# A state-space mixer on one Trainium2 core: silus and taps moved between slots, rounded output weights moved to GpSimd

## The chip, the cores and the metric

The kernel runs on one core of a Trainium2 chip. The metric is the device time of one launch in microseconds. The time before is 2786.01 us, the median of three runs (2781.27 to 2787.26).

## The reference

Four layers run one after the other on 1024 tokens (4 sequences of 256) of width 512: a selective scan, a mixture of experts, a mixer of the Mamba-2 kind and a feed-forward layer with block quantisation. Each is between layer norms and is added to the residual. The change touches the mixer only, which is cut here to what matters:

```python
proj = h @ in_proj_w.T                      # gate 8192, hidden 8192, B 1024, C 1024, dt 128
hBC = silu(causal_conv(hBC, conv_w, conv_b))  # 4 taps along time
hid, B, C = ...                             # 128 heads of 64; 8 groups of B and C, 128 wide
M = einsum('bcihn,bcjhn->bcijh', Ch, Bh) * L  # L = exp of differences of cumulated decays
Y = M @ (hid * dt) + D * hid                # (also across chunks)
yg = Y * silu(gate)
yg = yg * rsqrt(mean(yg * yg over a group) + EPS) * gnorm_w
out = residual + yg @ out_proj_w.T
```

The heads share B and C within a group: group g has 16 heads, which are 8 pairs of 2 heads, 128 channels a pair.

## The kernel before

The mixer (`mixer_groups`) goes over 72 steps: in each of 8 groups, first a step for B and C, then 8 steps, each for one pair (its hidden channels and its gate). The engines work through slots; in slot s the projections of step s are made, while the pair of step s - 1 is turned into y. With r = s % 9, slot r = 0 projects B and C of a new group and finishes the last pair of the old one, slot r = 1 projects the first pair and has no pair to finish, and slots r = 2 to 8 have both. In slots r = 1 to 4 of groups 1 to 7, TensorE also makes two tiles of 128 tokens of the group before's output (`out_tiles`), and in slots r = 5 to 8 two blocks of output weights are prepared for this group (`new_out_weights`): `wogh`, the weight times `gnorm_w`, rounded to the fp32r type, by ScalarE at L1674 (`high_weight`), and `wogl`, the rest, by VectorE at L1532 (`low_weight`). Every product in fp32r is three matmuls (L78, L79, L80) of rounded and remaining parts.

Each engine has a fixed order, written out in its loop over slots; semaphores tie them together.

TensorE in a slot with a pair: transposes of the pair's hidden channels (L1337, `turn`) for the first half of the tokens, projection 0 (12 matmuls of 512 columns), transposes for the second half, projection 1, the y matmuls of sequence 0 (L1354 and L1358), an out tile if there is one, projection 2, y of sequence 1, projection 3, the second out tile, then y of sequences 2 and 3. The four projections of a step go through three PSUM banks (`mg_pb`) in turn, so projection n waits until the bank's content of three projections ago was read: by the last tap for hidden, B and C, by the silu for the gate. One PSUM bank (`mg_tb`) serves both the transposes and the out tiles; each waits until the one before was emptied (`s_hc`, `s_acc`).

In slot r = 1 TensorE makes projections 0 and 1, the square sums of the finished group (L1380), the shared kernels (B times C of the group, L1372 and L1373, four sequences, in banks of `mg_gb` and `mg_py`), out tile, projection 2, half of projection 3, out tile, and the other half.

ScalarE makes the first tap of the convolution (L1608), the silus (L1618, L1625), the clamps of the decay differences for some sequences (L1639, L1640), the exponentials (L1652, L1658), the rounded halves `yh` (L1667) and `wogh`. The first tap of the second half waits until the product of the pair two steps back was read from the same buffer, by `gated(last, 1)` on GpSimd (L1268).

VectorE makes the other three taps (L1453, `taps`), the product with dt out of the transposes' bank (L1471, `times_step`), the kernels of the eight units of a pair (L1480, `kernel_of`: exponential times shared kernel), the remaining clamps (L1494, L1496), `skip` (L1503, y plus D times hidden), `low` (L1519), `low_weight`, and the sum of out tiles (L1527, `add`). The last y matmuls of a slot need kernels 6 and 7, which are behind `skip(p, 0)` and, in slot r = 0, behind the taps of C's first half.

GpSimd splits the projection weights of the next step (`split`: `wh` at L1256, `wl` at L1258), multiplies y with the silu of the gate (L1268, `gated`) and gathers squares (L1279, L1283, L1285). Its order in a slot is: `split(s + 1)`, second half of the pair before (`gated(last, 1)`, `squares(last, 1)`), first half of this slot's pair. In slot r = 1 the second half comes ahead of the split.

SyncE issues all loads: `mg_ws` (projection weights, one buffer), `mg_abc` (rows of decays), `mg_wos` (output weights, two buffers, L1248).

## Time and profile before

| what | value |
| --- | --- |
| median of 3 runs | 2786.01 us (2781.27 to 2787.26) |
| the profiled execution, its own time | 2787.32 us |
| its span on the core | 2785.5 us |
| granted TensorE clock, mean | 0.936 of full |
| the mixer's groups | about 915 to 2440 us |

The profile shows one execution. Its span runs from the first to the last instruction; the time has 1.8 us around it. Busy times are of instructions alone; waiting isn't busy. In a timeline an instruction's idle time before it, with the instruction that released it, stands in brackets. DVE is VectorE, ACT ScalarE, POOL GpSimd, PE TensorE.

### The profile page before, as it was taken

Reading aid. Unit: us, or ns where it says so; the run is one execution under the profiler, and the core shown is the slowest. Engines: PE = TensorE matmul, PEld = TensorE weight load, DVE = VectorE, ACT = ScalarE, POOL = GpSimd, SP = SyncE. Lnnn points to the kernel's source line nnn. Section 1 sums busy time; section 2 is a strip of 40 time slices with the busy share of each in tenths; the row PEclk is TensorE's granted clock in tenths of the full one; section 3 lists DMA queues with packets and bytes.
Section 4 is the critical chain, followed back from the end, with each engine's and each line's share of the span. In section 5 each row is a group of like instructions: output and inputs, shape, how many; then the busy total and the mean of one; then the engine's idle time right before and its main releaser. Section 6 shows DMA issues by size and latency. Waiting matters only on the chain. (4 is left out here: it accounts for less than half of the span.)

```text
span 2785.5 us, 35722 instructions
## 1 busy us (share of the span) xinstructions
PE 2347.3 (84%) x11172; PEld 1667.8 (60%) x11172; DVE 1986.3 (71%) x3392; ACT 1475.5 (53%) x3113; POOL 1240.7 (45%) x932
## 2 busy tenths in 40 slices
PE   5966667777342899999999999999999999888997
PEld 4531111225332667777767767767777777568996
DVE  4559999994426587686686685776765866778777
ACT  2344444443102596685695685765856956842221
POOL 1129989993000364353363462543543633641122
PEclk9989999998575899999999999999999999889999
DMA  2030030000131331231231221322322312220110
GB/s 78 24 122 0 0 121 0 0 0 31 57 121 64 94 124 60 72 114 54 74 117 48 87 92 53 105 73 65 108 64 68 112 53 75 82 77 24 46 46 31
DMA packets 117376, 183.57 MB, mean 66 GB/s; under 512 B 9760, under 2 KB 77728, under 8 KB 116192
## 3 DMA queue, kind: packets, MB, share of 16 engines
q1 hardware_dynamic: 117216, 181.55, 20.3%
q8 instruction: 86, 1.41, 0.2%
q14 instruction: 74, 0.61, 0.1%
HBM read 170.90 MB, written 10.62 MB: 65 GB/s over the span
## 5 line engine op out<-in xcount | busy, mean ns | idle before, releaser
L78 PE MATMUL mg_pb<-xT2h,mg_wh 128*128 128x512 f32 x1152 | 483.0, 419 | 18.2 <-POOL mg_wl L1258 18.2
L79 PE MATMUL mg_pb<-xT2l,mg_wh 128*128 128x512 f32 x1152 | 458.4, 398 | 0.0
L1268 POOL TENSOR_TENSOR mg_y<-mg_hT,mg_sg 128x512 f32<-128x512 f32 x128 | 175.5, 1371 | 634.5 <-DVE mg_hT L1503 634.5
L80 PE MATMUL mg_pb<-xT2h,mg_wl 128*128 128x512 f32 x1152 | 456.5, 396 | 0.0
L778 PE MATMUL ss_y<-ss_pr,cst 128*128 128x512 f32 x512 | 294.8, 664 | 125.4 <-POOL ss_pr L763 116.5
L763 POOL TENSOR_TENSOR ss_pr<-ss_h,ss_bc 128x512 f32<-128x512 f32 x256 | 328.4, 1287 | 38.6 <-DVE ss_h L731 29.3
L1453 DVE SCALAR_TENSOR_TENSOR mg_hT<-mg_pb,mg_cw,mg_hT 128x510 f32<-128x510 f32 (+2 forms) x432 | 314.2, 740 | 32.3 <-ACT mg_hT L1608 26.5
L1480 DVE TENSOR_TENSOR mg_m<-mg_gb,mg_cb 128x384 f32<-128x384 f32 x512 | 265.2, 549 | 74.7 <-ACT mg_gb L1658 72.1
L662 ACT ACTIVATE ss_da<-dt,ss_na 128x510 f32 (+1 forms) x256 | 175.9, 689 | 210.3 <-DVE ss_h L731 210.2
L778 PEld LDWEIGHTS ss_y<-ss_pr,cst 128*128 128x128 f32 x512 | 80.7, 194 | 338.0 <-POOL ss_pr L763 330.5
L78 PEld LDWEIGHTS mg_pb<-xT2h,mg_wh 128*128 128x128 f32 x1152 | 220.4, 191 | 80.2 <-issue 18.8
L80 PEld LDWEIGHTS mg_pb<-xT2h,mg_wl 128*128 128x128 f32 x1152 | 219.9, 191 | 52.2
L79 PEld LDWEIGHTS mg_pb<-xT2l,mg_wh 128*128 128x128 f32 x1152 | 220.6, 191 | 40.2
L1658 ACT ACTIVATE mg_gb<-mg_nd 128x256 f32<-128x256 f32 x512 | 190.0, 371 | 71.5 <-DVE mg_nd L1496 70.5
L731 DVE TENSOR_TENSOR_SCAN ss_h<-ss_da,ss_dbx 128x512 f32<-128x512 f32 x192 | 226.4, 1207 | 0.0
L1354 PE MATMUL mg_py<-mg_m,mg_hc 128*64 128x256 f32 x1024 | 170.2, 411 | 54.5 <-DVE mg_m L1480 54.4
L1527 DVE SCALAR_TENSOR_TENSOR acc<-mg_tb,mg_rs,acc 128x512 f32<-128x512 f32 x56 | 41.9, 748 | 211.7 <-PE mg_tb L80 211.7
L1652 ACT ACTIVATE mg_gb<-mg_abc,mg_tabs 128x128 f32<-128x128 f32 x512 | 182.7, 357 | 3.8 <-DVE mg_m L1480 2.1
L78 PE MATMUL mg_tb<-mg_wogh,mg_yh 128*128 128x512 f32 x448 | 180.0, 402 | 0.0
L1258 POOL TENSOR_TENSOR mg_wl<-mg_ws,mg_wh 128x1024 fp32r<-128x1024 f32 x72 | 176.0, 2445 | 6.0
L80 PE MATMUL mg_tb<-mg_wogh,mg_yl 128*128 128x512 f32 x448 | 177.0, 395 | 0.0
L1608 ACT ACTIVATE mg_hT<-mg_pb,mg_cbias,mg_cw 128x512 f32<-128x512 f32 x144 | 110.8, 770 | 124.7 <-PE mg_pb L80 113.7
(291 smaller groups left out, 5323.3 us busy)
## 6 DMA issues: line engine op xcount, KB each, us to landing
mg_abc<-acs_rows SPq DMA_DIRECT2D x256, 256.0 KB, 3.3
mg_ws<-in_w_in SPq DMA_DIRECT2D x72, 512.0 KB, 3.6
ss_bc<-bc_rows SPq DMA_DIRECT2D x16, 1024.0 KB, 8.5
mg_wos<-in_w_out SPq DMA_DIRECT2D x64, 256.0 KB, 4.0
ff_ws<-in_w SPq DMA_DIRECT2D x7, 1024.0 KB, 4.8
x<-in_x SPq DMA_DIRECT2D x16, 256.0 KB, 4.3
ip_ws<-in_w_in SPq DMA_DIRECT2D x8, 512.0 KB, 3.6
x_kept<-x SPq DMA_DIRECT2D x2, 2048.0 KB, 7.2
```

The lines of the kernel that those rows point to most:

```text
L78: pe.matmul(out, lhs[0], rhs[0], start=start, stop=False)
L79: pe.matmul(out, lhs[0], rhs[1], start=False, stop=False)
L80: return pe.matmul(out, lhs[1], rhs[0], start=False, stop=stop)
L662: act.activation(da[n % RA][:].rearrange("p (b t) -> p b t", t=SEQ)[:, :, 1:], src[:, :, 1:], ACT.Exp, scale=na[:, bass.ds(k, 1), n:n + 1] ...
L731: dve.tensor_tensor_scan(hh[n % RA][:], da[n % RA][:], src[:], 0.0, ALU.mult, ALU.add).then_inc(s_h, 1)
L763: pool.tensor_tensor(pr[n % 2][:], hh[n % RA][:], bcb[:, NST + n, :], ALU.mult).then_inc(s_pr, 1)
L778: pe.matmul(yb[:], ident, pr[n % 2][:], start=False, stop=n == NST - 1).then_inc(s_y, 1)
L1258: pool.tensor_tensor(wl[s % 2][:], ws[:], wh[s % 2][:].bitcast(F32), ALU.subtract).then_inc(s_lo, 1)
L1453: i = dve.scalar_tensor_tensor(out=d3, in0=s3, scalar=w[:, TAPS - 1 - k:TAPS - k], in1=d3, op0=ALU.mult, op1=ALU.add)
L1480: dve.tensor_tensor(mm[u % 4][:], gb[u % 2][:, 0:BLK], cbt[:, u // 2, :], ALU.mult).then_inc(s_m, 1)
L1652: act.activation(gb[u % 2][:, 2 * P:BLK], abc[(BATCH * p + b) % 3][:, hh, P:SEQ], ACT.Exp, bias=tabs[g % 2][:, 2, 2 * b, 2 * q + hh:2 * q ...
L1658: act.activation(gb[u % 2][:, 0:2 * P], nd[u % 4][:], ACT.Exp, scale=1.0 if by_dve(p, b) else -1.0).then_inc(s_e, 1)
```

## The change

Two things change in the mixer.

First, the work on B and C. In slot r = 0, VectorE makes only the taps of B (the two halves 0 and 1); the taps of C (2 and 3) are made at the start of slot r = 1, around `low` of the first out tile. ScalarE makes all first taps in slot r = 0, those of C behind the exponentials 6 and 7, and all four silus of B and C in slot r = 1. TensorE makes the shared kernels in slot r = 1 behind projection 2 instead of behind projection 1, and projection 3 in one piece ahead of the second out tile; VectorE takes them (`shared_out`) behind `low` of the second out tile.

Second, `wogh` is made by GpSimd, by a multiplication with the column of `gnorm_w` and an addition of 0. Its first weight of a slot stands ahead of `split(s + 1)`, the second between `split(s + 1)` and `gated(last, 1)`.

```diff
--- before.py
+++ after.py
@@ -1284,14 +1284,26 @@
                     pool.wait_ge(s_sqt, n + 1)
                     pool.tensor_tensor(ssq[:, t], ssq[:, t], sq[:], ALU.add).then_inc(s_sq, 1)
 
+                def high_weight(w):
+                    pool.wait_ge(s_wo[w % 2], 16 * (w // 2) + 16)
+                    if w >= PAIRS:
+                        pool.wait_ge(s_out, w // PAIRS * MT)
+                    pool.tensor_scalar(wogh[:, w % PAIRS, :], wos[w % 2][:], gn[:, w:w + 1], 0.0, ALU.mult, ALU.add
+                                       ).then_inc(s_wog, 1)
+
+                pool.wait_ge(s_tab, 64)
                 split(0)
                 for s in range(NSTEP + 2):
-                    last = turned_pair(s - 1) if s else None
+                    last, ow = turned_pair(s - 1) if s else None, new_out_weights(s)
+                    if ow:
+                        high_weight(ow[0])
                     if last is not None and (s % PS == 1 or s > NSTEP):
                         gated(last, 1)
                         squares(last, 1)
                     if s + 1 < NSTEP:
                         split(s + 1)
+                    if ow:
+                        high_weight(ow[1])
                     if last is not None and not (s % PS == 1 or s > NSTEP):
                         gated(last, 1)
                         squares(last, 1)
@@ -1423,16 +1435,15 @@
                     proj(s, 1, 1)
                     if outs:
                         square_sums(s // PS - 1)
-                    if not is_bc(s):
-                        shared_kernels(s // PS)
-                    if outs:
                         out_tile(*outs[0])
                     proj(s, 2, 0)
                     proj(s, 2, 1)
+                    if not is_bc(s):
+                        shared_kernels(s // PS)
                     proj(s, 3, 0)
+                    proj(s, 3, 1)
                     if outs:
                         out_tile(*outs[1])
-                    proj(s, 3, 1)
                 square_sums(NG - 1)
 
             @block.vector
@@ -1567,30 +1578,29 @@
                             add(*outs[0])
                             low(*outs[1])
                         skip(p, 0)
-                        if bc:
-                            taps(s, 2)
                         kernel_of(p, 6)
                         kernel_of(p, 7)
                         if outs:
                             add(*outs[1])
                         skip(p, 1)
-                        if bc:
-                            taps(s, 3)
                         continue
                     if bc:
-                        for j in range(4):
-                            taps(s, j)
+                        taps(s, 0)
+                        taps(s, 1)
                         continue
+                    taps(s - 1, 2)
                     if outs:
                         low(*outs[0])
+                    taps(s - 1, 3)
                     taps(s, 0)
                     if outs:
                         scales(outs[0][0])
                     taps(s, 1)
-                    shared_out(s // PS)
                     if outs:
                         add(*outs[0])
                         low(*outs[1])
+                    shared_out(s // PS)
+                    if outs:
                         add(*outs[1])
                 scales(NG - 1)
                 dve.wait_ge(s_rs, NG)
@@ -1667,45 +1677,32 @@
                         ins = act.activation(yh[:, q0:q1, :], yb[:, r0:r0 + q1 - q0, m * P:(m + 1) * P], ACT.Copy)
                     ins.then_inc(s_yh, 1)
 
-                def high_weight(w):
-                    act.wait_ge(s_wo[w % 2], 16 * (w // 2) + 16)
-                    if w >= PAIRS:
-                        act.wait_ge(s_out, w // PAIRS * MT)
-                    act.activation(wogh[:, w % PAIRS, :], wos[w % 2][:], ACT.Copy, scale=gn[:, w:w + 1]).then_inc(s_wog, 1)
-
                 def root(g):
                     act.wait_ge(s_ss, g + 1)
                     act.activation(sd[:], gb[1][:, BLK:BLK + MT], ACT.Sqrt, bias=eps[:, 2:3], scale=1.0 / GRP
                                    ).then_inc(s_sd, 1)
 
                 for s in range(NSTEP + 1):
-                    p, outs, ow = turned_pair(s), out_tiles(s), new_out_weights(s)
+                    p, outs = turned_pair(s), out_tiles(s)
                     bc = is_bc(s)
                     if p is not None:
                         decay(p, 0)
                         decay(p, 1)
                         if outs:
                             high(*outs[0])
-                        if ow:
-                            high_weight(ow[0])
                         first_tap(s, 0)
                         decay(p, 2)
                         decay(p, 3)
                         first_tap(s, 1)
                         decay(p, 4)
                         decay(p, 5)
-                        if ow:
-                            high_weight(ow[1])
-                        if bc:
-                            first_tap(s, 2)
                         if outs:
                             high(*outs[1])
                         decay(p, 6)
                         decay(p, 7)
-                        if bc and s < NSTEP:
+                        if bc:
+                            first_tap(s, 2)
                             first_tap(s, 3)
-                            for j in range(4):
-                                silu(s, j)
                             continue
                         silu(s, 0)
                         silu(s, 1)
@@ -1715,16 +1712,17 @@
                     if bc:
                         for j in range(4):
                             first_tap(s, j)
-                        for j in range(4):
-                            silu(s, j)
                         continue
                     if outs:
                         high(*outs[0])
+                    silu(s - 1, 0)
+                    silu(s - 1, 1)
+                    silu(s - 1, 2)
                     first_tap(s, 0)
+                    silu(s - 1, 3)
+                    first_tap(s, 1)
                     if outs:
                         root(outs[0][0])
-                    first_tap(s, 1)
-                    if outs:
                         high(*outs[1])
                     silu(s, 0)
                     silu(s, 1)
```

## Rows read from the trace of the kernel before

**Rows 1.** The page: busy time of each engine, and TensorE's clock in 40 slices.

```profile
PE 2347.3 (84%) x11172; PEld 1667.8 (60%) x11172; DVE 1986.3 (71%) x3392; ACT 1475.5 (53%) x3113; POOL 1240.7 (45%) x932
...
PEclk9989999998575899999999999999999999889999
```

**Rows 2.** Busy time of each engine, 1200 to 1300 us; then granted clock, DMA share, GB/s.

```profile
1200.00:1300.00 100.00, 93.70 (x496) 70.48 (x495) 77.12 (x129) 72.44 (x164) 54.49 (x40) 0.97 0.27 86
```

**Rows 3.** Who waited for whom, 1000 to 2450 us: total us, times, longest.

```profile
PE mg_py L1354 <- DVE mg_m L1480: 52.5, 35, 3.8
...
ACT mg_hT L1608 <- POOL mg_y L1268: 10.1, 23, 0.5
```

**Rows 4.** TensorE's timeline: start us, us, instruction, [idle before it <-releaser].

```profile
1251.20 0.65 PE L1354 MATMUL mg_py<-mg_m,mg_hc 128*64 128x256 f32 x4 [0.85 <-DVE mg_m L1480]
...
1270.75 1.12 PE L1354 MATMUL mg_py<-mg_m,mg_hc 128*64 128x256 f32 x4 [3.78 <-DVE mg_m L1480]
...
1272.23 0.80 PE L78 MATMUL mg_pb<-xT2h,mg_wh 128*128 128x512 f32 x1
...
1276.21 0.40 PE L78 MATMUL mg_pb<-xT2h,mg_wh 128*128 128x512 f32 x1
...
1279.65 1.84 PE L1380 MATMUL mg_gb<-cst,mg_ssq 128*128 128x1 f32 x16
...
1299.13 0.40 PE L80 MATMUL mg_tb<-mg_wogh,mg_yl 128*128 128x512 f32 x1
...
1300.76 0.60 PE L1337 MATMUL mg_tb<-cst,mg_hT 128*128 128x128 f32 x4
...
2417.72 0.65 PE L1354 MATMUL mg_py<-mg_m,mg_hc 128*64 128x256 f32 x4
```

**Rows 5.** VectorE's timeline, slots r = 0 and r = 1.

```profile
1252.15 0.75 DVE L1503 SCALAR_TENSOR_TENSOR mg_hT<-mg_hT,mg_dp,mg_py 128x512 f32<-128x512 f32 x1 [1.00 <-PE mg_py L1358]
...
1266.81 0.74 DVE L1503 SCALAR_TENSOR_TENSOR mg_hT<-mg_hT,mg_dp,mg_py 128x512 f32<-128x512 f32 x1
1267.46 2.30 DVE L1453 SCALAR_TENSOR_TENSOR mg_sg<-mg_pb,mg_cw,mg_sg 128x510 f32<-128x510 f32 x3
1269.68 1.01 DVE L1480 TENSOR_TENSOR mg_m<-mg_gb,mg_cb 128x384 f32<-128x384 f32 x2
...
1277.08 4.24 DVE L1519 TENSOR_TENSOR mg_yl<-mg_y,mg_yh 128x256 fp32r<-128x256 f32 x2 [1.74 <-ACT mg_yh L1667]
...
1299.57 0.75 DVE L1527 SCALAR_TENSOR_TENSOR acc<-mg_tb,mg_rs,acc 128x512 f32<-128x512 f32 x1 [7.18 <-PE mg_tb L80]
```

**Rows 6.** Timelines of GpSimd, VectorE and ScalarE in a weight slot, r = 8.

```profile
1237.38 1.06 POOL L1256 TENSOR_SCALAR mg_wh<-mg_ws 128x1024 fp32r<-128x1024 f32 x1
1238.52 2.40 POOL L1258 TENSOR_TENSOR mg_wl<-mg_ws,mg_wh 128x1024 fp32r<-128x1024 f32 x1
1240.87 1.75 POOL L1268 TENSOR_TENSOR mg_y<-mg_hT,mg_sg 128x512 f32<-128x512 f32 x1
...
1239.31 2.16 DVE L1532 SCALAR_TENSOR_TENSOR mg_wogl<-mg_wos,mg_gn,mg_wogh 128x512 fp32r<-128x512 f32 x1
...
1245.67 1.01 DVE L1480 TENSOR_TENSOR mg_m<-mg_gb,mg_cb 128x384 f32<-128x384 f32 x2
...
1242.72 0.78 ACT L1608 ACTIVATE mg_hT<-mg_pb,mg_cbias,mg_cw 128x512 f32<-128x512 f32 x1 [0.44 <-POOL mg_y L1268]
...
1245.46 0.37 ACT L1658 ACTIVATE mg_gb<-mg_nd 128x256 f32<-128x256 f32 x1
```

**Rows 7.** GpSimd's timeline at the end of slot r = 0.

```profile
1267.62 1.26 POOL L1268 TENSOR_TENSOR mg_y<-mg_hT,mg_sg 128x512 f32<-128x512 f32 x1 [6.26 <-DVE mg_hT L1503]
...
1270.08 1.27 POOL L1285 TENSOR_TENSOR mg_ssq<-mg_ssq,mg_sq 128x512 f32<-128x512 f32 x1
```

**Rows 8.** GpSimd's instruction groups, whole span: xcount, busy us, mean ns, idle before.

```profile
L1256 POOL TENSOR_SCALAR mg_wh<-mg_ws 128x1024 fp32r<-128x1024 f32 x72 | 75.7, 1052 | 199.6 <-PE mg_pb L80 158.1 <-DMA mg_ws<-in_w_in 41.6
...
L1035 POOL MEMSET st_go<- 128x4 f32 x1 | 0.1, 104 | 0.1
```

## The prediction, made blind

> **What bounds the kernel now.** I read the page first. TensorE is busy 84% of the span, the other engines 45 to 71%, and its clock is at full level over most of the second half [rows 1]. The mixer's groups fill about 915 to 2440 us of the span. In a stretch of 100 us there, TensorE is busy 93.7 us and no other engine 80 [rows 2]. So TensorE sets the time, and only its gaps, and any microsecond at the lower of its two levels (1.2 GHz instead of 2.4), can be won. The table of waits names one large reason for the gaps: the last y matmul of a slot (L1354) waits for the kernels that VectorE makes at L1480, 52.5 us in 35 waits [rows 3]. The timeline divides them. Seven waits of about 3.76 us (26 us) end the slots with r = 0; 24 waits of about 0.84 us (20 us) end the slots with r = 5 to 8, in which output weights are made (four in group 0; r = 6, 7, 8 in groups 1 to 6; r = 6 and 7 in group 7). One row of each kind stands in [rows 4]. After a long wait TensorE is at the lower level: its nine projection matmuls from 1272.23 to 1276.21 us come every 0.44 us, the next 15, to 1279.65, every 0.23 [rows 4].
>
> **Part 1: C's taps leave slot r = 0.** VectorE ends skip(p, 0) at 1267.46, then makes the three taps of C's first half (2.2 us), and only then kernels 6 and 7, from 1269.68 to 1270.69; TensorE starts 0.06 later [rows 4, 5]. Without the taps the kernels start at 1267.46 and the last y matmuls at 1268.53. The gap shrinks by 2.2 us to 1.56. A gap of 0.85 leaves the clock up and one of 3.78 doesn't [rows 4]. I take 1.56 as harmless, by the nearer one; the rivals have the other end.
>
> I now follow slot r = 1 from there, at full clock. The y matmuls take 0.80 (1251.20 to the transposes at 1252.00), 24 projection matmuls 24 x 0.233 = 5.6, and everything from the square sums on, out tiles and shared kernels included, 1300.76 - 1279.65 = 21.1 [rows 4]. Their sum doesn't change with their order. What changes are the waits:
> - Projection 1 of the slot needs the bank whose taps are now late. skip(p, 1) starts 0.95 after the last y matmuls, as at 1252.15 after 1251.20 [rows 4, 5], so at 1269.48; the moved taps run from 1270.14 to 1272.36. TensorE is there at 1269.33 + 2.8 = 1272.1. Cost 0.3.
> - Square sums need GpSimd's three instructions on the second half of the last pair. GpSimd is busy with the first half until 1270.08 + 1.27 = 1271.35; its three take 3.73 (1267.62 to 1271.35) [rows 7], so alone 1275.1. But low of the first out tile now asks at 1272.4, between them. That is a subtraction of two SBUF tiles; at 1277.08 two such took 4.24 us beside GpSimd's work [rows 5], so the two engines shut each other out. With its 1.2 us slipped in, GpSimd ends at 1276.3; TensorE is there at 1275.2. Cost 1.0, between 0 (no collision) and 1.2.
> - The second out tile now ends the slot. Before, six projection matmuls (1299.37 to 1300.76) covered the add that empties its bank: add starts at 1299.57 and takes 0.75 [rows 4, 5]. After, the transposes of the next slot wait for it: 1300.4 instead of 1299.37. Cost 1.0.
> - The silus of B and C and the four first taps stay ahead of the shared kernels by several us, since these now follow the first out tile and projection 2 (8.4 us); VectorE's waits for them fall into time in which it idles now (7.18 us before the row at 1299.57 [rows 5]). Cost 0. The cover is the first out tile: without it the shared kernels would wait for silu(s - 1, 3).
>
> So slot r = 2 starts at 1268.53 + 0.80 + 5.6 + 21.1 + 0.3 + 1.0 + 1.0 = 1298.3 instead of 1300.76: 2.4 us won per group, 3.4 without the collision. It happens seven times: 17 us, up to 24. Group 0 has no out tile and wins nothing; at its start B and C come in the same order on VectorE.
>
> **Part 2: rounded output weights by GpSimd.** ScalarE loses 64 x 0.71 us, which is worth little: behind its first weight it waits for GpSimd (0.44 us, [rows 6]), behind the second for VectorE's clamps. GpSimd gains two instructions in each of 32 slots. The trace has none of their size. The same operation on 1024 columns takes 1.05 us, an instruction on 4 columns 0.10 [rows 8]; so 512 columns take 0.53 (half) to 0.58 (fixed part kept). I take d = 0.575. The far bound is 1.05, an instruction no shorter for half the columns. The Trainium skill (GPSIMD Engine Reference, 3.1) gives GpSimd two software dispatch steps and puts VectorE's dispatch alone at 156 ns; an estimate with 0.16 as the fixed part would be 0.60, and the sum 1 us worse.
>
> Now a weight slot [rows 6]. GpSimd has wh at 1237.38, wl at 1238.52, and then gated(last, 1) at 1240.87, which takes 1.75 instead of 1.26 because VectorE's low_weight holds it off. gated ends at 1242.62, and ScalarE's first tap of the second half, which overwrites what gated reads, starts 0.10 later. Then come clamps and exponentials; the last one ends at 1245.83, and VectorE's kernel 5 (the second of the pair at 1245.67) starts at 1246.13. The slack between the two is 0.30, or 0.24 with the usual 0.06 of handover. After the change both weights stand ahead of gated(last, 1): it ends 2d = 1.15 later, and kernel 5 is 1.15 - 0.24 = 0.91 later. The other path is shorter: low_weight waits for wl to end (2.16 us instead of its own 0.74), and wl moves by d = 0.575 only. Behind kernel 5 VectorE has clamps, taps, the second low_weight, skip and kernels 6 and 7 without a gap up to TensorE's wait. So each of the 24 stalls grows by 0.91, to 1.75: 21.8 us.
>
> The other eight weight slots keep their time: r = 5 of groups 1 to 7, where the first weight must now wait for the last out tile but ScalarE waits for projection 1 anyway, and the last slot, which has no split and shows no stall today (2417.72, [rows 4]). The DMAs are the same; a weight is asked for 1 to 2 us earlier than by ScalarE, inside the time it has now. The next load of projection weights starts 0.6 us later, up to 4.6 in r = 5; it has most of a slot to spare. GpSimd's added wait for the tables at its start covers what split(0) waits for anyway. Cost 0.
>
> **Sum.** 21.8 - 17.0 = +4.8 us. The profiled execution took 2787.3 (span 2785.5); the median of the runs shown is 1.3 lower, so 2786.0 + 4.8 = 2790.8, rounded to 2791. With d of 0.53 to 0.65 the loss is 0.82 to 1.06 per slot (20 to 25 us) and the gain 12 (further small waits at the first out tile) to 24: 2782 to 2799.
>
> **Rival A, the port goes to VectorE first.** VectorE asks for the port at 1239.31, 0.8 after wl starts. If d is over 0.79, wl hasn't begun by then; low_weight goes first, wl waits about 0.5, and gated ends 1.6 (d = 0.8) to 2.1 (d = 1.05) later: 1.35 to 1.83 per slot, 32 to 44 us, so 2801 to 2813, about 2806. For it: the scalar is read from a column of a tile here, not given as a constant as at L1256. Against: a time proportional to columns puts d well below. The Trainium skill (SBUF — State Buffer, two separate sides) has the first to start keep the shared pair for its whole instruction, which would turn the order at this same point; that the wl row and low_weight end together agrees.
>
> **Rival B, faster: GpSimd's delay is absorbed.** The place is the handover from gated(last, 1) to the first tap. If ScalarE, relieved of 0.6 us ahead of it, or VectorE's order hides the delay, the growth per slot is 0 to 0.5 and the gain of part 1 stays: 2769 to 2781, about 2775. It decides at a growth of 17 / 24 = 0.71 us per slot. Against: ScalarE already waits for gated in 23 places, 10.1 us [rows 3], so relief ahead of it only lengthens that wait.
>
> **Rival C, the clock falls anyway.** Gaps of 1.6, 0.3 and 1.0 now lie within 8 us. The fall costs 8.90 - 6.4 = 2.5 us a time (1270.75 to 1279.65 against 0.80 + 5.6, [rows 4]); seven times is 17 us and brings the time to about 2808. Against: the gaps of 0.85, one a slot, don't do it, and matmuls fill the time between.
>
> **How the numbers follow.** The forecast has 0.47, rival A 0.18, rival B 0.27, rival C 0.08. Both signs hold weight, so the likeliest case's own range is 2782 to 2799. The range to hold 8 in 10 reaches over B and most of A: 2770 to 2809. A measurement of this kernel tells 0.2% (5.6 us) from nothing. Faster by more: B, 0.26. Within it: a good half of the forecast, 0.32. Slower: the rest of the forecast, A and C, 0.42.
>
> **What would show it.** Right: TensorE's wait ahead of the last y matmuls about 1.5 us at r = 0 with the clock up, and about 1.75 in 24 weight slots; ScalarE's wait for gated (L1268) up from 0.4 to over 2 us; a new gap of 1 us ahead of L1337 in slot r = 2, and one ahead of L1380; GpSimd's new group at 0.55 to 0.6 us. Wrong: stalls of 0.8 unchanged in the weight slots, a new group over 0.8 us, or long rows of 0.63 at r = 0.

## The result and the profile after

| | before | after |
|---|---|---|
| median of 5 runs | 2786.01 us (2781.27 to 2787.26) | 2800.01 us (2797.43 to 2803.30) |
| ratio, 95% interval | | 1.0054 (1.0040 to 1.0069) |
| the profiled execution | 2787.32, span 2785.5 | 2800.01, span 2798.2 |

The change makes the kernel 0.5% slower. The forecast was 2791.0 within 2770 to 2809: the sign and the range hold, and the size is three times too small.

The page of the kernel after, to be set beside [rows 1]:

```profile
PE 2351.4 (84%) x11172; PEld 1667.0 (60%) x11172; DVE 1952.2 (70%) x3392; ACT 1440.2 (51%) x3049; POOL 1289.4 (46%) x996
...
PEclk9989999998575999999999999999999999989999
```

TensorE's busy time is what it was (2351 against 2347 us). ScalarE lost its 64 instructions, GpSimd has 64 more and 49 us more work, and the span grew by 12.7 us. So the time is again in TensorE's gaps, and in what its clock does around them. The table of waits, 1000 to 2450 us (who waited for whom: total us, times, longest):

```profile
PE mg_py L1366 <- DVE mg_m L1491: 51.1, 31, 2.7
ACT mg_hT L1618 <- POOL mg_y L1268: 43.2, 23, 2.3
...
PE mg_tb L1349 <- DVE acc L1538: 6.5, 7, 0.9
...
PE mg_gb L1392 <- POOL mg_ssq L1285: 2.8, 7, 0.5
PE mg_pb L78 <- DVE mg_sg L1464: 0.6, 4, 0.2
```

TensorE's wait for kernels has the same sum as in [rows 3] (51.1 against 52.5 us), but made up differently: nothing reaches 3.8 us any more, and the many small ones have grown. ScalarE's wait for gated went from 10.1 to 43.2 us, over 23 places in both. The last three rows are the bill for part 1: the kernel before has no such waits in slots r = 0 and 1 (its one wait for square sums, 5.0 us, stands behind the last group).

To see where each microsecond lies I measured slots. A slot runs from the first transposes (L1337 before, L1349 after) behind one pair's last y matmuls to those behind the next pair's. The table is worked out from their starts in TensorE's timeline, in us:

| stretch | before | after | difference |
|---|---|---|---|
| up to the first projection | 915.3 | 912.3 | -3.0 |
| from there to slot r = 2 of group 0 | 27.3 | 26.5 | -0.8 |
| the 24 weight slots that stall | 399.4 (16.64 each) | 428.2 (17.84) | +28.8 |
| slots r = 0 and 1 together, 7 times | 340.5 (48.65) | 329.7 (47.09) | -10.9 |
| all other slots, the last one too | 736.0 | 736.0 | 0.0 |
| behind them | 367.0 | 365.6 | -1.4 |
| sum | 2785.5 | 2798.2 | +12.7 |

Part 2 costs 28.8 us, and part 1 wins 10.9 in slots r = 0 and 1. The 0.8 us at the start of group 0 isn't shown to be the change's: that stretch took 25.9 to 27.4 us over the kernels of this study, and e4 and e9, which have part 1, took 27.3 and 27.4. The first stretch holds nothing of the change, and over the thirteen kernels of this study it came out anywhere from 909 to 916 us; it is scatter of single executions. The last stretch was 365.4 to 365.7 in all but two kernels (before and e8_low_late, 367.0 and 366.7), which I can't explain. Single spans carry up to 7 us of this, so the mechanisms below are read from slots, and the medians only check them. The slots too are those of one profiled execution of each kernel.

### The profile page after: what moved, and what is told of

Read it like the earlier page. It is cut to its first block and busy times, and to the rows that moved or that the text cites. A ratio compares the mean times of both kernels' runs of the same rounds, so it can differ in the third digit from the quotient of the medians.

```text
span 2798.2 us, 35723 instructions
## 1 busy us (share of the span) xinstructions
PE 2351.4 (84%) x11172; PEld 1667.0 (60%) x11172; DVE 1952.2 (70%) x3392; ACT 1440.2 (51%) x3049; POOL 1289.4 (46%) x996
## 5 line engine op out<-in xcount | busy, mean ns | idle before, releaser
L78 PE MATMUL mg_pb<-xT2h,mg_wh 128*128 128x512 f32 x1152 | 483.6, 420 | 18.7 <-POOL mg_wl L1258 17.7
L1268 POOL TENSOR_TENSOR mg_y<-mg_hT,mg_sg 128x512 f32<-128x512 f32 x128 | 164.9, 1289 | 623.1 <-DVE mg_hT L1514 623.1
L78 PEld LDWEIGHTS mg_pb<-xT2h,mg_wh 128*128 128x128 f32 x1152 | 220.1, 191 | 82.2 <-issue 18.5
L1258 POOL TENSOR_TENSOR mg_wl<-mg_ws,mg_wh 128x1024 fp32r<-128x1024 f32 x72 | 183.8, 2553 | 6.0
```

The lines of the kernel that those rows point to most:

```text
L78: pe.matmul(out, lhs[0], rhs[0], start=start, stop=False)
L1258: pool.tensor_tensor(wl[s % 2][:], ws[:], wh[s % 2][:].bitcast(F32), ALU.subtract).then_inc(s_lo, 1)
```

## The experiments

All ratios are to the kernel before, whose median in each batch lay between 2783.7 and 2786.3 us. "Slots" are a weight slot's mean over the 24, then the mean of r = 0 and 1 together over the 7, worked out as above.

| run | median us | ratio (95%) | slots |
|---|---|---|---|
| e1_taps_only | 2767.6 | 0.9954 (0.9940 to 0.9967) | 16.64; 46.65 |
| e2_weights_only | 2806.5 | 1.0084 (1.0070 to 1.0098) | 17.88; 47.27 |
| e3_second_late | 2786.6 | 1.0011 (1.0001 to 1.0020) | 17.14; 47.31 |
| e4_constant | 2788.4 | 1.0023 (1.0012 to 1.0034) | 17.55; 46.42 |
| e5_cover | 2757.7 | 0.9915 (0.9901 to 0.9928) | 16.64; 45.35 |
| e6_gated_first | 2762.0 | 0.9917 (0.9903 to 0.9930) | 15.91; 47.38 |
| e7_change_gated_first | 2785.7 | 1.0008 (0.9999 to 1.0017) | 16.66; 48.45 |
| e8_low_late | 2765.2 | 0.9931 (0.9917 to 0.9944) | 16.63; 45.36 |
| e9_first_in_slots_6_to_8 | 2745.3 | 0.9854 (0.9841 to 0.9868) | 15.91; 46.02 |
| e10_weights_in_idle | 2762.2 | 0.9915 (0.9900 to 0.9930) | 16.70; 45.79 |
| e11_row_first | 2758.9 | 0.9897 (0.9880 to 0.9914) | 16.37; 46.24 |

### Each part alone

**e1_taps_only** is the kernel after with the rounded weights back on ScalarE:

```diff
 # gpsimd
-                    if ow:
-                        high_weight(ow[0])
 ...
 # scalar
+                        if ow:
+                            high_weight(ow[0])
                         first_tap(s, 0)
```

> The changed kernel with the rounded weights back on ScalarE: part 1 alone. Theory (the two parts don't touch each other): slots r = 0 and r = 1 of each group take 46.4 to 47.7 us as in the changed kernel, weight slots 16.64 as in the kernel before, so about 11 us less than before: 2775. Rival (ScalarE needs the relief for the moved silus, so part 1 is worth nothing alone): 2784 or more, with longer waits on ScalarE in slot r = 1.

**e2_weights_only** is the kernel before with only high_weight moved to GpSimd.

> The kernel before with only the rounded weights on GpSimd: part 2 alone. Theory: 24 weight slots grow by 1.2 us each, slots r = 0 and 1 keep their 48.8 us: 2786 + 29 = 2815. Rival (the growth comes from both parts together, or half of it from noise ahead of the mixer): 2800 or less.

Measured: the weight slots of e1 are before's (16.64) and those of e2 are after's (17.88), so part 2 alone makes the stall. Part 1 alone makes the kernel 0.5% faster. Both kernels came out some 8 us below what was expected of them (2767.6 for 2775, 2806.5 for 2815). In the slots the two parts aren't additive: part 1 wins 14.0 us where nothing else changed (340.5 to 326.5 in slots r = 0 and 1) and 1.2 on top of part 2 (330.9 to 329.7). The medians, each against that of the kernel before in its own batch, say 16.1 and 8.7 us, with about 4 us of uncertainty on each ratio. The reason is the clock. TensorE's timeline of e2, in three groups:

```profile
1278.33 0.65 PE L1366 MATMUL mg_py<-mg_m,mg_hc 128*64 128x256 f32 x4 [2.43 <-DVE mg_m L1492]
...
1286.24 1.84 PE L1392 MATMUL mg_gb<-cst,mg_ssq 128*128 128x1 f32 x16
...
1475.40 0.65 PE L1366 MATMUL mg_py<-mg_m,mg_hc 128*64 128x256 f32 x4 [3.75 <-DVE mg_m L1492]
1477.10 0.63 PE L78 MATMUL mg_pb<-xT2h,mg_wh 128*128 128x512 f32 x1
...
1483.38 1.84 PE L1392 MATMUL mg_gb<-cst,mg_ssq 128*128 128x1 f32 x16
...
1653.01 0.65 PE L1366 MATMUL mg_py<-mg_m,mg_hc 128*64 128x256 f32 x4 [2.02 <-DVE mg_m L1492]
...
1655.09 0.63 PE L80 MATMUL mg_pb<-xT2h,mg_wl 128*128 128x512 f32 x1
...
1672.73 0.65 PE L1366 MATMUL mg_py<-mg_m,mg_hc 128*64 128x256 f32 x4 [2.35 <-DVE mg_m L1492]
...
1679.14 1.84 PE L1392 MATMUL mg_gb<-cst,mg_ssq 128*128 128x1 f32 x16
```

From the last y matmuls to the square sums the same work takes 7.91, 7.98 and 6.41 us; in the kernel before it took 8.90 [rows 4] (8.90 to 8.96 in six groups, 7.95 in group 0). The rows of 0.63 us are matmuls at the lower level (1.2 GHz), those of 0.39 at the higher. The level falls in all three groups, but not in the same place. In the second it falls behind the gap of 3.75 us. In the third it falls at the start of slot r = 0 (the row at 1655.09), behind the stall of 2.02 us with which part 2 ends slot r = 8, and is up again at 1657.95. The slow projections fill time in which TensorE would have waited for VectorE: the gap ahead of the last y matmuls is 2.35 us instead of 3.75, nothing falls behind it, and slots r = 0 and 1 take 46.45 us instead of 48.8. The first group has some of both. So the fall behind the gap costs 2.5 us in six groups of the kernel before, 1.5 in five groups of e2 and nothing in its other two, and moving the weights gave back 9.7 us in slots r = 0 and 1 (340.5 to 330.9).

The other timelines show the same. A fall directly behind a weight slot's stall comes in 9 of 24 places in the kernel after and in 10 of 24 in e2 (stalls of 2.0 us), in 2 of 24 in e4 below (1.75 us), and in none in e3 (1.35 us), e1 and the kernel before (0.84 us).

### What makes the weight slot longer

**e3_second_late** puts the second rounded weight behind gated(last, 1) and its squares on GpSimd; **e4_constant** gives the instruction the constant 1.0 instead of a column of gnorm_w, which leaves gnorm_w out of the rounded weights:

```diff
 # e3
-                    if ow:
-                        high_weight(ow[1])
                     if last is not None and not (s % PS == 1 or s > NSTEP):
                         gated(last, 1)
                         squares(last, 1)
+                    if ow:
+                        high_weight(ow[1])
 # e4
-  pool.tensor_scalar(wogh[:, w % PAIRS, :], wos[w % 2][:], gn[:, w:w + 1], 0.0, ALU.mult, ALU.add
+  pool.tensor_scalar(wogh[:, w % PAIRS, :], wos[w % 2][:], 1.0, 0.0, ALU.mult, ALU.add
```

> The changed kernel with GpSimd's second weight of a slot behind squares(last, 1) instead of ahead of gated(last, 1). Theory (gated, then ScalarE's first tap, sets the growth): gated ends only one weight (0.66 us) later than in the kernel before, which would give 0.66 - 0.24 = 0.42 us a slot; VectorE's low_weight, moved by the first weight, is then the longer path with about 0.65. So 0.65 instead of 1.2 in 24 slots: 13 us less than the changed kernel, about 2787. Rival (low_weight's wait for the port sets the growth already): no change, 2800.

> The changed kernel with GpSimd's weights multiplied by the constant 1.0 instead of gnorm_w's column; the rounded weights then lack gnorm_w. It measures why the instruction takes 0.69 us where I expected 0.575. Theory (reading the scalar from a tile costs about 0.1): it takes 0.58 to 0.60, growth per slot falls by 2 x 0.1, so 24 x 0.2 = 5 us less, 2795. Rival (the fixed part of an instruction is larger than the memset's 0.10): 0.69 as before, 2800.

A weight slot of the kernel after (start us, us, instruction), to be read with [rows 6]: TensorE, GpSimd, VectorE.

```profile
1218.72 0.65 PE L1366 MATMUL mg_py<-mg_m,mg_hc 128*64 128x256 f32 x4 [2.03 <-DVE mg_m L1491]
...
1221.55 0.70 POOL L1291 TENSOR_SCALAR mg_wogh<-mg_wos,mg_gn 128x512 fp32r<-128x512 f32 x1
1222.21 1.05 POOL L1256 TENSOR_SCALAR mg_wh<-mg_ws 128x1024 fp32r<-128x1024 f32 x1
1223.35 2.95 POOL L1258 TENSOR_TENSOR mg_wl<-mg_ws,mg_wh 128x1024 fp32r<-128x1024 f32 x1
1226.29 0.68 POOL L1291 TENSOR_SCALAR mg_wogh<-mg_wos,mg_gn 128x512 fp32r<-128x512 f32 x1
1226.95 1.28 POOL L1268 TENSOR_TENSOR mg_y<-mg_hT,mg_sg 128x512 f32<-128x512 f32 x1
...
1223.30 0.74 DVE L1543 SCALAR_TENSOR_TENSOR mg_wogl<-mg_wos,mg_gn,mg_wogh 128x512 fp32r<-128x512 f32 x1
```

And the y matmuls ahead of the slot of [rows 6], from the kernel before:

```profile
1234.56 0.65 PE L1354 MATMUL mg_py<-mg_m,mg_hc 128*64 128x256 f32 x4 [0.83 <-DVE mg_m L1480]
```

A weight is 0.68 to 0.70 us long, and the next instruction starts 0.66 behind its start: that is d, not 0.575. Everything is best counted from the y matmuls. gated ends 1228.23 - 1218.72 = 9.51 us behind them, before 1242.62 - 1234.56 = 8.06: 1.45 later. Less the slack of 0.24 that makes 1.21, and the slots grew by 1.20. Of the 1.45, 1.32 are the two weights. The rest is rival A's event: low_weight now comes first, 0.05 ahead of wl. wl takes 0.55 more for it (2.95 against 2.40), and gated no longer meets low_weight (1.28 against 1.75), so the flip costs about 0.1. Rival A had the right picture and the wrong threshold: wl starts 0.66 later, as it should (4.63 behind the y matmuls against 3.96), but VectorE also asks 0.17 earlier (4.58 against 4.75), so the order turns near d = 0.62, not 0.79.

e3 and e4 test that the chain through gated, and no other, sets the slot. In e3 one weight is left ahead of gated and low_weight is first as well:

```profile
1236.14 0.65 PE L1366 MATMUL mg_py<-mg_m,mg_hc 128*64 128x256 f32 x4 [1.34 <-DVE mg_m L1491]
...
1240.78 2.94 POOL L1258 TENSOR_TENSOR mg_wl<-mg_ws,mg_wh 128x1024 fp32r<-128x1024 f32 x1
1243.68 1.28 POOL L1268 TENSOR_TENSOR mg_y<-mg_hT,mg_sg 128x512 f32<-128x512 f32 x1
```

gated ends 8.82 behind the y matmuls, 0.76 later than before; 0.76 - 0.24 = 0.52, and the slots grew by 0.50. low_weight took 0.74 there, against 2.16 before, and still the slot is longer, so it isn't low_weight. In e4 the weight takes 0.62 (the second one 1.06, held off by low_weight as gated was before), the old order holds (wl 2.40), and gated ends 9.22 behind: 1.16 - 0.24 = 0.92, growth 0.91. Three kernels, three delays, one slack.

The totals are weaker evidence. e3 came out where it was expected (13.4 us below the kernel after), but by other terms: the weight slots grew by 0.50 each and not 0.65, which won 16.7 us, and slots r = 0 and 1 gave 1.5 back. e4 was expected at 2795 and took 2788.4: the weight slots won 7.1 us, and slots r = 0 and 1 another 4.7.

### What the second out tile covered

**e5_cover** is e1 with the second half of projection 3 behind the second out tile again:

```diff
                     proj(s, 3, 0)
-                    proj(s, 3, 1)
                     if outs:
                         out_tile(*outs[1])
+                    proj(s, 3, 1)
```

> Part 1 alone (run e1), with the second half of projection 3 behind the second out tile again, as in the kernel before. It tests the wait for the add, 0.94 us ahead of the transposes in slot r = 2, which e1 and the changed kernel have seven times. Theory: the wait goes, 7 x 0.94 = 6.6 us less than e1's 2767.6: 2761. Rival (the transposes then wait for something else as long, or the clock falls more often): 2766 or more.

Measured: slots r = 0 and 1 take 45.05 to 45.25 us where no clock falls, against 46.12 to 46.32 in e1: 1.07 won per group, and the wait for the add (6.5 us, 7 times) is gone from the table of waits. The weight slots stay at 16.64. By the profiled executions e5 is 9.0 us shorter than e1 in slots r = 0 and 1, since the clock fell in one group instead of two as well.

### The order on GpSimd

Since gated(last, 1) alone sets the stall, I moved it ahead of the split in e5, with its squares (**e6_gated_first**), and did the same to the kernel after, with both weights ahead of it (**e7_change_gated_first**):

```diff
-                    if last is not None and (s % PS == 1 or s > NSTEP):
+                    if last is not None:
                         gated(last, 1)
                         squares(last, 1)
                     if s + 1 < NSTEP:
                         split(s + 1)
-                    if last is not None and not (s % PS == 1 or s > NSTEP):
-                        gated(last, 1)
-                        squares(last, 1)
```

> e5 with GpSimd's gated(last, 1) and squares(last, 1) ahead of split(s + 1) in every slot, weights on ScalarE. Theory (a weight slot of the kernel before is set by ScalarE's first tap waiting for gated, and by low_weight waiting for the long wl): gated ends at 4.1 us of the slot instead of 8.1, low_weight waits for a short squares instead of wl and ends 1.0 us earlier; kernel 5 ends 0.7 earlier, so 24 slots take about 15.95 instead of 16.64: 16 us less than e5. Rival (VectorE's clamps now meet wl late in the slot, or ScalarE's table loads bound kernel 0 and with it the slot): weight slots stay at 16.6, no change to e5.

> The changed kernel with GpSimd's order: both weights, gated(last, 1), squares(last, 1), split(s + 1). GpSimd does the same work as in the changed kernel. Theory (not the added work but its place ahead of gated costs the 1.2 us): gated ends at 5.4 us of the slot, long before ScalarE wants it; the clamps of sequence 3 then wait some 0.4 for wl. Weight slots of about 16.5 instead of 17.83, 24 x 1.35 = 32 us less than the changed kernel's 2800: 2768. Rival (GpSimd's added work and port time cost wherever they stand): 2790 or more.

The stall is gone in e6 (15.87 us a slot, the same as a slot without a split). The time didn't follow: 16 us less than e5 was expected, and it took 4 more. Slots r = 0 and 1 are 2.0 us longer than in e5, group 0's slots 2 to 4 too, and those of the later groups 0.7. VectorE's timeline of e6 in slot r = 0 shows why:

```profile
1251.95 1.39 DVE L1490 TENSOR_SCALAR mg_nd<-mg_abc,mg_tabs 128x128 f32<-128x128 f32 x1
1253.26 1.09 DVE L1492 TENSOR_SCALAR mg_nd<-mg_abc,mg_tabs 128x128 f32<-128x128 f32 x1
1254.27 0.27 DVE L1490 TENSOR_SCALAR mg_nd<-mg_abc,mg_tabs 128x128 f32<-128x128 f32 x1
1254.46 2.42 DVE L1492 TENSOR_SCALAR mg_nd<-mg_abc,mg_tabs 128x128 f32<-128x128 f32 x1
```

These are the clamps, 0.28 us each when alone. The last one begins 0.10 after wl (1254.36 to 1256.80 us on GpSimd) and ends with it. The four take 4.9 us; with the split first, in e9, they take 3.5, and slot r = 0 is 1.35 longer in e6. The rest of the 2.0 is the clock, which fell in four groups of e6 and in one of e5. In weight slots low_weight is in the place of these clamps. e7 shows the same trade on the kernel after: 16.66 us instead of 17.84 in the weight slots, 1.4 more in slots r = 0 and 1, and 14 us less in all. Neither expectation was met: the order gave 28.5 us back in the weight slots, which vary from 16.2 to 17.7, and took 9.4 in slots r = 0 and 1 and 4.8 in slots 2 to 4 (2785.7 us, where 2768 was expected and the rival had 2790 or more). So the place of the added work costs more than the work, but the order has a price of its own. Is low_weight's own place worth anything?

**e8_low_late** is e5 with the first low_weight moved next to the second.

> e5 with VectorE's first low_weight of a slot moved behind the clamps and taps, next to the second, where GpSimd idles: it takes 0.74 instead of 2.16. Theory (the slot is set by VectorE's chain behind kernel 5, to which low_weight's 0.66 is now added, while ScalarE's exponentials keep kernel 5 from starting over 0.8 earlier): 16.5 instead of 16.64 a slot, 3 us less than e5. Rival (low_weight's wait of 1.4 us is the whole stall): 15.8 a slot, 20 us less than e5.

No: it took 2765.2 us, 7 more than e5 and not 3 less. The weight slots stay as they are (16.60), and seven slots r = 5 grow by 0.66. gated no longer meets low_weight (1.29 us instead of 1.76), but the two low_weights in a row lengthen VectorE's last stretch by as much.

**e9_first_in_slots_6_to_8** is e5 with gated(last, 1) ahead of the split in the slots 6 to 8 alone: `if last is not None and (s % PS in (1, 6, 7, 8) or s > NSTEP)`, and the reverse behind the split.

> e5_cover, with GpSimd's gating and squares of the previous pair's second half ahead of the split of the input weights only in the slots r = 6, 7 and 8. There e6 took 15.87 us a slot instead of 16.64, which is 24 x 0.77 = 18.5 us; what e6 paid for it stood in the slots r = 2 to 4 (80.85 instead of 80.15 us) and r = 0 and 1 (46.4 to 48.2 instead of 45.05 to 45.25). Theory (the delay of the gated product by the split is the whole of the stall in the weight slots, and the later split is harmful only where a slot has no gap to spare): 15.87 in the slots 6 to 8, 80.15 and 45.1 in the others, so 2757.7 - 18.5 = 2739 us, ratio 0.984. Rival (the split made later in slot r = 8 also delays the projection of the shared step, so that what is won is given back in slot r = 0): slots r = 0 and 1 at 46.5 or more, 2750 us or more.

This is the best version, 41 us faster than the kernel before by the medians and 55 faster than the kernel after. The slots are as expected: 15.86 to 15.89 in all 23 places (group 0's slot 5 is left out and keeps 16.63; my 24 was one too many), 80.14 to 80.17 in slots 2 to 4. GpSimd's timeline in a weight slot of e9:

```profile
1227.90 1.29 POOL L1285 TENSOR_TENSOR mg_ssq<-mg_ssq,mg_sq 128x512 f32<-128x512 f32 x1
1229.14 1.29 POOL L1268 TENSOR_TENSOR mg_y<-mg_hT,mg_sg 128x512 f32<-128x512 f32 x1
...
1233.24 1.03 POOL L1256 TENSOR_SCALAR mg_wh<-mg_ws 128x1024 fp32r<-128x1024 f32 x1
1234.35 2.41 POOL L1258 TENSOR_TENSOR mg_wl<-mg_ws,mg_wh 128x1024 fp32r<-128x1024 f32 x1
```

The median is 6 us above the expected 2739. In the profiled execution four of seven groups took 46.6 to 46.8 us in slots r = 0 and 1, the others 45.0 to 45.3; in e5 one did. TensorE's timeline of e9 has the reason, in the first out tile:

```profile
1266.81 1.95 PE L1380 MATMUL mg_gb<-cst,mg_ssq 128*128 128x1 f32 x16 [0.30 <-POOL mg_ssq L1285]
...
1269.17 0.39 PE L80 MATMUL mg_tb<-mg_wogh,mg_yl 128*128 128x512 f32 x1
1269.40 0.59 PE L78 MATMUL mg_tb<-mg_wogh,mg_yh 128*128 128x512 f32 x1
1269.78 0.63 PE L79 MATMUL mg_tb<-mg_wogl,mg_yh 128*128 128x512 f32 x1
```

The level fell there, 9.9 us behind the gap of 1.52 us ahead of the last y matmuls, with waits of 0.15 and 0.30 us between.

### Does the weight belong on GpSimd at all?

**e10_weights_in_idle** is e9 with both weights on GpSimd at the start of its slot, ahead of gated. **e11_row_first** adds to that one row load ahead of the load of projection weights on SP's queue:

```diff
                         load_rows(BATCH * p + 3)
+                        load_rows(BATCH * p + 4)
                     if s + 2 < NSTEP:
                         load_w(s + 2)
```

> The kernel of e9_first_in_slots_6_to_8 with the rounded output weights on GpSimd, both at the start of its slot, ahead of the gating, where GpSimd idles for 4.5 us in e6. Theory (it is the place in GpSimd's order that cost the change its time, not the engine): the two instructions of 0.69 us end before the gated product's inputs are there, so nothing of the chain to the kernels moves by more than the part of 1.38 us that does not fit into the idle time; slots 6 to 8 at 15.87 to 16.2 us, time within 8 us of e9's. Rival (GpSimd is too full with the weights, or its longer use of the port it shares with VectorE slows VectorE's chain): slots of 16.5 to 17.3 us as in e7, which is 15 to 34 us more than e9.

> The kernel of e10_weights_in_idle, with one more of the next pair's four row loads (the first one that ScalarE reads in the next slot) ahead of the load of projection weights on SP's queue. In e10 that load of weights waits for the end of wl, which the two rounded weights make late (issued at 1243.14 us, the three rows behind it from 1243.52), and ScalarE's first clamps of a slot then wait for the rows' transfer: 11.9 us in 19 waits, none in e9. The rounded weights themselves wait for their own transfer, issued behind the rows: 8.7 us in 13 waits. Theory (the weight slots of e10, 16.2 to 17.3 us instead of e9's 15.87, are long because of transfers issued behind that wait, not because GpSimd is full): ScalarE's wait for the rows is gone, at most 1 us is left; slots 6 to 8 at 15.9 to 16.4 us, so 8 to 16 us less than e10's 2762: 2746 to 2754. Rival (GpSimd's work itself or the port holds VectorE off): slots stay at 16.2 to 17.3 and the time within 4 us of e10's.

By its total e10 fits the rival (16.9 us more than e9, where the rival had 15 to 34). The waits point elsewhere: ScalarE's wait for gated is gone from the table of waits. e10's weight slots are 16.2 to 18.4 us, and its table of waits has two rows that e9's hasn't:

```profile
ACT mg_nd L1648 <- DMA mg_abc<-acs_rows: 11.9, 19, 0.9
POOL mg_wogh L1291 <- DMA mg_wos<-in_w_out: 8.7, 13, 2.0
```

SP issues the rows behind a load that waits for wl to end, and wl is now last on GpSimd. With one row ahead of that load (e11), ScalarE's wait is gone, the other is 1.5 us in 5, and 16 of the 24 slots come to 16.16 to 16.20. So transfers are part of it: e11 wins back 8.1 of the 19.1 us by which e10's 24 are longer than e9's. The total, 2758.9, missed the expected 2746 to 2754 and lies within 4 us of e10's, as the rival had it; five groups of its profiled execution had the clock's fall, three of e10's. What stays in most slots, 0.31 us, is one clamp held off by wl, and that is the rival's cause; the rest, group 0's slot 5 with 18.5 us above all, I didn't follow up. VectorE's timeline of e11:

```profile
1243.38 0.73 DVE L1505 TENSOR_SCALAR mg_nd<-mg_abc,mg_tabs 128x128 f32<-128x128 f32 x1
1244.04 0.28 DVE L1507 TENSOR_SCALAR mg_nd<-mg_abc,mg_tabs 128x128 f32<-128x128 f32 x1
```

GpSimd's wl ran until 1244.03 and held the first clamp off by 0.45 us. In e9, where wl ends 0.8 us ahead of it, that clamp takes 0.28. No place tried for the weights on GpSimd was as good as ScalarE.

## Why the prediction was right or wrong

- **What bounds the kernel** was right. The others' busy time moved by 34 to 49 us and the span by the change in TensorE's gaps.
- **Part 1, the gap at r = 0.** Forecast 1.56 us; 1.52 to 1.56 in all groups of e1 and 1.57 in three of the kernel after: the three taps were all of it. In the other four groups of the kernel after it is 0.1 us, because the level had fallen at or shortly before the start of slot r = 0. TensorE's timeline of the kernel after:

```profile
1271.56 0.65 PE L1366 MATMUL mg_py<-mg_m,mg_hc 128*64 128x256 f32 x4 [1.57 <-DVE mg_m L1491]
...
1275.53 0.50 PE L78 MATMUL mg_pb<-xT2h,mg_wh 128*128 128x512 f32 x1 [0.15 <-DVE mg_sg L1464]
...
1278.86 1.95 PE L1392 MATMUL mg_gb<-cst,mg_ssq 128*128 128x1 f32 x16 [0.32 <-POOL mg_ssq L1285]
...
1282.44 0.63 PE L78 MATMUL mg_tb<-mg_wogh,mg_yh 128*128 128x512 f32 x1
...
1302.71 0.63 PE L1349 MATMUL mg_tb<-cst,mg_hT 128*128 128x128 f32 x4 [0.94 <-DVE acc L1538]
...
1451.24 0.65 PE L1366 MATMUL mg_py<-mg_m,mg_hc 128*64 128x256 f32 x4 [2.05 <-DVE mg_m L1491]
...
1453.04 0.63 PE L79 MATMUL mg_pb<-xT2l,mg_wh 128*128 128x512 f32 x1
```

- **The three new waits.** The bank of projection 1: 0.3 forecast, 0.15 measured. The add at the slot's end: 1.0 and 0.94. The square sums: 1.0 and 0.32 (up to 0.5). The last was mis-sized because I let low's whole 1.2 us slip in between GpSimd's instructions; the last of GpSimd's three took 1.88 instead of 1.30, so 0.6 was lost, part of it covered. From start to start, where no level falls, the waits cost more than the brackets say: 7.30 to 7.52 us from the last y matmuls to the square sums in e1 against 6.4 in e2's third group, and 22.28 behind them against 21.11. That is 0.9 to 1.1 us where 1.3 was forecast, and 1.2 where 1.0 was.
- **The clock in slot r = 1.** This step failed. I took 1.56 as harmless "by the nearer one", and directly behind the gap it is. But in four of seven groups (1, 3, 5 and 6) the level fell some 10 us later, in the first out tile (the row of 0.63 at 1282.44). I had followed the stretch up to the square sums only. Each such fall costs 1.55 us: 23.84 us from the square sums to slot r = 2 instead of 22.28. That is rival C in part, 1.55 us four times instead of 2.5 seven times, and its 6.2 us are what part 1 missed (10.9 instead of 17.0). Without a fall these two slots take 46.1 to 46.3 us in e1, 2.4 less than the 48.65 before, which is the forecast.
- **The other three groups** (0, 2 and 4) aren't free of a fall either: the level fell at the start of slot r = 0, behind part 2's stall (2.05 us at 1451.24, the row of 0.63 at 1453.04), which costs 0.2 us, since TensorE would have waited later in that slot anyway, and no second fall followed. So part 2 changed the clock in part 1's slots. The prediction let the weight stall grow to 1.75 us and asked nothing about the level behind it, and its own sign of being wrong, long rows of 0.63 at r = 0, came true in this way.
- **What part 1 was worth** is nearly all clock, which the prediction's sum held (8.90 against 0.80 + 5.6) but didn't name. From start to start, the gap gives 2.2 us and the new waits take 2.1 to 2.3; what stays is the 2.5 us of the fall behind the old gap, which no longer comes. e2's groups 3 and 5 show how much that part goes by circumstances: before's own order, with the level falling where it costs nothing, takes 46.4 us.
- **Part 2, the mechanism** was right at each handover: gated later by 2d, less 0.24; the path of low_weight no matter; ScalarE's wait for gated up by (43.2 - 10.1) / 23 = 1.4 us a place; r = 5 of groups 1 to 7 unchanged. e3 and e4 show it. One reading was loose: low_weight doesn't end together with wl but 0.55 us behind it (1241.47 against 1240.92, [rows 6]), most of its own 0.74.
- **Part 2, the size** failed most. d = 0.575 came from half a 1024-column instruction; it is 0.66. Twice 0.085 is 0.17 a slot, the order's flip 0.1: growth 1.20 instead of 0.91, and 24 x 0.29 = 7.0 us. e4 parts the error in d: without the column of a tile the instruction takes 0.62, so 0.07 is the column. The rest is a fixed part of 0.19 us (1.05 for 1024 columns, 0.62 for 512), where the row on 4 columns suggested 0.10. The Trainium skill's figure for VectorE's dispatch (GPSIMD Engine Reference, 3.1) had given an estimate of 0.60; the trace puts d above that too.
- **The other eight weight slots** kept their time.
- **The sum.** +4.8 forecast. +7.0 for d, +6.1 for part 1 (10.9 instead of 17.0) and -0.8 at the start of group 0 make +17.1; the two stretches outside the mixer give 4.4 back, to +12.7. The median difference is 14.0.
- **Rival B** fell: nothing absorbs the delay, since ScalarE waits for gated in 23 places, 1.9 us each. **Rival A**'s event came, at d = 0.66 already, and cost 0.1 us a slot, not the 0.4 and more of its price, most of which was d itself.

What stays open is when the late fall comes. e1, e3 and e4 have the same slots r = 0 and 1, and it came in two, five and one of seven groups. What differs is how long the weight slots ahead are, and in e4 one group had its fall at the start of slot r = 0 instead. I saw no row that decides it for the others.

## What to carry to other kernels

Before giving an idle engine more work, look for the instruction on it for which another engine waits, and count what the new work puts ahead of it: here 2 x 0.66 us ahead of one gated product cost 29 us, and moving that product ahead of 3.5 us of other work in the right slots won 18 in those slots (12 by the medians). A wait removed on a bound engine is worth its length plus what the clock does behind it, and the second can be the larger and the less certain half; read it over the whole stretch that follows, in several groups. A fall of the clock costs nothing where the engine would have waited anyway, so a stall made longer in one place can make another place faster. And where a transfer's issue waits for an engine's last instruction, an instruction that moves back on that engine makes late all that is queued behind the transfer.

## What the runs showed of the hardware

- GpSimd's multiplication of 128x512 f32 by one scalar takes 0.62 us with a constant and 0.69 with a column of a tile (1.05 for 1024 columns and a constant).
- VectorE's small instructions can be held off by GpSimd for nearly the whole of a long one: a clamp on 128x128 took 2.42 us instead of 0.28 and ended 0.08 us behind GpSimd's wl, low_weight 2.16 instead of 0.74, ending 0.55 behind it [rows 6]. The reverse costs as much as is left of the shorter one: low_weight ahead of wl cost wl 0.55 us. The one that began earlier was the undelayed one, by as little as 0.05 us. The Trainium skill (SBUF — State Buffer, two separate sides) has the first to start keep the shared pair, and the trace agrees.
- TensorE's fall to the lower level after a gap isn't fixed by the gap alone. Behind 3.8 us it cost 2.5 us in six groups of the kernel before and 1.5 in e2. Behind 2.0 us it came at once in 9 of 24 places (after) and 10 of 24 (e2), behind 1.75 us in 2 of 24 (e4), behind 1.35 and 0.84 us in none (e3, e1, before). In the slots with a gap of 1.5 to 1.6 us it came some 10 us behind it, in one to five of seven groups, for 1.55 us each.
- A fall costs only what the engine had no wait to spare for: eight projections at the lower level in e2's slot r = 0 (group 3) made the slot 0.2 us longer and the gap behind them 1.4 us shorter.
